# Mixer A: issuing the next chunk's matmuls ahead of the accumulation, with a lag of three states

## What is computed

```python
x_part, z = jnp.split(xn @ in_proj_w.T, 2, axis=-1)
u = jax.nn.silu(conv(x_part))                     # depthwise, 4 taps, 256 channels
dt, Bm, Cm = jnp.split(u @ x_proj_w.T, [8, 24], axis=-1)   # 8 ranks, 16 states
delta = jax.nn.softplus(dt @ dt_proj_w.T + dt_proj_b)
h = exp(delta * A) * h + delta * B * u            # for each step, channel and state
y = sum_over_states(h * C) + u * D
out = (y * jax.nn.silu(z)) @ out_proj_w.T
```

## Time and profile before

| | |
|---|---|
| median of 3 runs | 1151.61 us (1148.47 to 1152.67) |
| the profiled execution | 1151.89 us, span 1150.1 us |
| busy share of the span | PE 88%, DVE 65%, ScalarE 53%, POOL 50% |
| mean granted PE clock | 0.942 of full speed |
| mixer A | about 41 to 317 us of the span |

### The profile page before, as it was taken

One profiled execution on the slowest core, in us unless ns is written; L12 is line 12 of the kernel. 1 busy time (PEld: TensorE's weight loads), 2 busy tenths in 40 slices (PEclk: granted clock), 3 DMA queues, 4 the chain that ended last, 5 costly groups with the idle time before them and its releaser, 6 DMA issues. The chain is left out here.

```text
span 1150.1 us, 16414 instructions
## 1 busy us (share of the span) xinstructions
PE 1012.2 (88%) x4830; PEld 713.5 (62%) x4830; DVE 752.6 (65%) x1167; ACT 609.5 (53%) x1154; POOL 575.6 (50%) x455
## 2 busy tenths in 40 slices
PE   5988888868787989999999688896897899999997
PEld 2323323222255769999998345654575699999996
DVE  4788787998839755555555496655478555555555
ACT  5565463754254445555555586667542455555553
POOL 2378576685600687633741474621001887444732
PEclk9889889999979999999999987998988999999999
DMA  4222121222141214311111300000320133111103
GB/s 136 56 65 65 46 64 56 65 75 62 39 130 47 62 28 102 108 53 53 45 35 39 87 1 1 1 1 1 103 74 32 46 89 81 53 53 60 54 26 115
DMA packets 57248, 66.41 MB, mean 58 GB/s; under 512 B 6088, under 2 KB 40656, under 8 KB 57168
## 3 DMA queue, kind: packets, MB, share of 16 engines
q1 hardware_dynamic: 52176, 55.13, 15.9%
q0 software_dynamic: 4992, 10.23, 3.6%
HBM read 54.86 MB, written 10.49 MB: 57 GB/s over the span
## 5 line engine op out<-in xcount | busy, mean ns | idle before, releaser
L685 POOL TENSOR_TENSOR a_hc<-a_h,a_c_sb 128x512 f32<-128x512 f32 x128 | 160.1, 1267 | 94.3 <-DVE a_h L606 86.3
L417 PE MATMUL ps<-a_hc,eye 128*128 128x512 f32 x256 | 147.6, 684 | 24.1 <-POOL a_hc L685 23.6
L531 ACT ACTIVATE ps<-a_delta,a_neg_a 128x512 f32<-128x512 f32 x128 | 87.6, 688 | 111.4 <-DVE a_h L606 111.1
L417 PEld LDWEIGHTS ps<-a_hc,eye 128*128 128x128 f32 x256 | 45.1, 205 | 89.7 <-POOL a_hc L685 64.5
L590 DVE TENSOR_TENSOR a_b_u<-a_du,ps 128x1024 f32<-128x1024 f32 x64 | 77.2, 1206 | 35.9 <-PE ps L404 35.6
L877 POOL CAST g_ring_rounded<-g_ring 128x1876 fp32r<-128x1876 f32 x8 | 14.1, 1761 | 151.5 <-DVE g_table L1392 102.1
L606 DVE TENSOR_TENSOR_SCAN a_h<-ps,a_state,a_b_u 128x512 f32<-128x512 f32 x64 | 78.9, 1266 | 0.0
L1021 PE MATMUL ps<-g_ring_rounded,g_q_hi_rounded 128*128 x312 | 77.0, 337 | 0.0
L1021 PE MATMUL ps<-f_ring_rounded,f_q_hi_rounded 128*128 x312 | 77.0, 337 | 0.0
L606 DVE TENSOR_TENSOR_SCAN a_h<-ps,a_b_u 128x512 f32<-128x512 f32 x64 | 75.2, 1208 | 0.8 <-ACT ps L531 0.6
L877 POOL CAST f_ring_rounded<-f_ring 128x1876 fp32r<-128x1876 f32 x8 | 14.1, 1760 | 114.4 <-DVE f_table L1392 70.4
(11 more groups left out here) (450 smaller groups left out, 2865.8 us busy)
## 6 DMA issues: line engine op xcount, KB each, us to landing
a_c_sb<-c_rows SPq DMA_DIRECT2D x64, 256.0 KB, 3.3
f_ring<-in_gu SPq DMA_DIRECT2D x16, 469.0 KB, 4.5
g_ring<-in_gu SPq DMA_DIRECT2D x16, 469.0 KB, 4.4
f_ring<-in_dn SPq DMA_DIRECT2D x8, 512.0 KB, 6.6
g_ring<-in_dn SPq DMA_DIRECT2D x8, 512.0 KB, 5.7
xn_rows<-f_work SPq DMA_DIRECT2D x8, 256.0 KB, 2.6
f_rows<-token_rows SPq DMA_DIRECT2D x8, 256.0 KB, 5.0
xn_rows<-g_work SPq DMA_DIRECT2D x8, 256.0 KB, 2.6
```

The lines of the kernel that those rows point to most:

```text
L417: nc.tensor.matmul(ps[:, Y + f, :], k.eye[:, :], hc[:, s % DEPTH, :], start=False, stop=(n == NST - 1)).then_inc(y_added, 1)
L531: nc.scalar.activation(ps[:, A + m % NA, :], delta[:, f, cols(g)], ACT.Exp, scale=neg_a[:, f, n:n + 1])\
L685: nc.gpsimd.tensor_tensor(hc[:, s % DEPTH, :], h[:, s % DEPTH, :], c_sb[:, i % RING, :], ALU.mult)\
```

## The change

PE issues the next chunk's matmuls (`between`) ahead of the accumulation, and the accumulation runs three states behind the broadcasts instead of two. The product buffers `hc` become six, and POOL waits for the addition six steps before. DVE's gate comes after state 0 of the next chunk instead of state 1. Everything else is as before.

```diff
--- before.py
+++ after.py
@@ -255,6 +255,8 @@
 
     STEPS = NST * FT
     DEPTH = 4
+    WAITING = 6
+    LAG = 3
     RING = 4
     w_in = sb("w_in", [P, 2 * DI])
     w_tap = sb("w_tap", [P, FT, TAPS, P])
@@ -272,7 +274,7 @@
     c_rows = nc.dram_tensor("c_rows", (NST, T), F32, kind="Internal").ap()
     decayed_in = sb("b_u", [P, DEPTH, CH])
     h = sb("h", [P, DEPTH, CH])
-    hc = sb("hc", [P, DEPTH, CH])
+    hc = sb("hc", [P, WAITING, CH])
     c_sb = sb("c_sb", [P, RING, CH])
     state = sb("state", [P, STEPS])
     yz = sb("yz", [P, FT, CH])
@@ -414,7 +416,7 @@
                         u_done(g)
                         nc.tensor.matmul(ps[:, Y + f, :], skip[:, f, :], u[:, f, cols(g)], start=True, stop=False)
                     pe.wait_ge(hc_ready, s + 1)
-                    nc.tensor.matmul(ps[:, Y + f, :], k.eye[:, :], hc[:, s % DEPTH, :],
+                    nc.tensor.matmul(ps[:, Y + f, :], k.eye[:, :], hc[:, s % WAITING, :],
                                      start=False, stop=(n == NST - 1)).then_inc(y_added, 1)
 
             norm.of_tensor(pe)
@@ -439,11 +441,11 @@
             pe.wait_ge(z_first, FT)
             for m in range(NST * NCH):
                 broadcast(m)
-                if m >= 2:
-                    accumulate(m - 2)
                 between(*divmod(m, NST))
-            accumulate(NST * NCH - 2)
-            accumulate(NST * NCH - 1)
+                if m >= LAG:
+                    accumulate(m - LAG)
+            for m in range(NST * NCH - LAG, NST * NCH):
+                accumulate(m)
             in_turn(NCH, PROJECT)
 
         @block.scalar
@@ -607,7 +609,7 @@
                                              initial, ALU.mult, ALU.add).then_inc(scanned, 1)
 
             def between(g, n):
-                if g and n == 1:
+                if g and n == 0:
                     gate(g - 1)
                 if g and n == 4:
                     add(g - 1)
@@ -680,9 +682,9 @@
                     i = g * NST + n
                     if f == 0:
                         pool.wait_ge(c_loaded[i % RING], (i // RING + 1) * 16)
-                    if m >= DEPTH:
-                        pool.wait_ge(y_added, m - DEPTH + 1)
-                    nc.gpsimd.tensor_tensor(hc[:, s % DEPTH, :], h[:, s % DEPTH, :], c_sb[:, i % RING, :], ALU.mult)\
+                    if m >= WAITING:
+                        pool.wait_ge(y_added, m - WAITING + 1)
+                    nc.gpsimd.tensor_tensor(hc[:, m % WAITING, :], h[:, s % DEPTH, :], c_sb[:, i % RING, :], ALU.mult)\
                         .then_inc(hc_ready, 1)
                     if g + 1 < NCH:
                         if s == 21:
```

## The result

The changed kernel takes 1167.78 us (median of 4 runs, 1165.75 to 1170.99), the one before 1150.18 us (4 runs). The ratio is 1.0154, with a 95% interval of 1.0121 to 1.0187: slower by 17.6 us. The forecast was 1161.3 us with a range of 1143 to 1170, slower with a chance of 0.56; the measured time lies in that range, and 0.8 us above the 1156 to 1167 that the forecast gave its own mechanism.

A forecast was written before the change was run, and what follows sets the result against it. DVE was taken to bound mixer A. Its idle time was to go from 36.2 to 45.6 us, 9.4 us more, which added to 1151.9 us gave 1161.3 us, range 1143 to 1170.

The forecast's parts named there:

- Start: Start of chunk 0: DVE idles 1.5 us in place of 2.5 us before its fourth product.
- First dt projection and what follows it: Middle of three chunks: accumulation delays the broadcast, 2.24 us plus 2.5 us for slow clock, booked 4.8 us each.
- Second z projection: Three chunks: accumulation behind the wait for ScalarE's copy of z, 7.9 us plus 1.4 us each for clock.
- Gates: First two chunk boundaries: gate waits for the last state's accumulation, 4.55 us plus 2.5 us for clock, 7.05 us each.
- Output projection: Iteration 4 behind two boundaries: projection and accumulation delay the broadcast, 0.85 us plus 0.9 us for clock each.
- Third boundary: Last chunk boundary: no convolution in the gate's way, so zero wait.
- rival 2: PE slow after every gap, for as long as the chain lasts: 56.0 us of DVE idle, 1171.7 us; chance 0.12.
- Gaps over 4 us are slow: PE gaps over 4 us bring half pace for a mean 5.05 us, 2.5 us lost each.
- rival 1: Clock holds at 2.4 GHz at gate, dt and z projections: 26.9 us of DVE idle, 1142.6 us; chance 0.18.
- rival 3: Removed and new waits pay for each other: 34.6 us of DVE idle, 1150.3 us; chance 0.2.
- Rival 4: PE takes the accumulation in its slack, leaving only gains, up to 20.0 us at the boundaries: 1132 us; chance 0.03.

The follow-up runs named there:

- e2: Changed kernel with PE's old order, accumulation ahead of the next chunk's matmuls; lag three, six buffers, early gate kept: 1259.15 us, 0.9856 of the kernel before.
- e10: The kernel of e2 run again, beside its neighbours of another group: 1257.72 us, 0.9854 of the kernel before.
- e7: Changed kernel with four added matmuls ahead of PE's wait for each first dt projection, order unchanged: 1155.32 us, 1.0046 of the kernel before.
- e12: The changed kernel run again without edits, beside the other experiments: 1295.50 us, 1.0157 of the kernel before.
- e6: Changed kernel with the accumulation issued ahead of the second z projection in that iteration: 1162.11 us, 1.0099 of the kernel before.
- e4: Kernel before with six product buffers instead of four and nothing else: 1277.46 us, 0.9997 of the kernel before.
- e8: Changed kernel with the gate back after state 1: 1158.30 us, 1.0071 of the kernel before.
- e5: Changed kernel with the accumulation issued ahead of the second convolution in that iteration (state 2 of each chunk): 1152.32 us, 0.9999 of the kernel before.

## Why the prediction was right, and where it was off

**The direction and the cause held.** The forecast's mechanism, a ready accumulation between a late read of bank O and the broadcast, is shown by e2 and e10: order restored, nothing else, and the kernel goes from 1.6% slower to 1.5% faster. The clock as second factor is shown by e7.

**Terms of the sum, forecast against the first profile.** Start 1.5 us, measured 2.1. First dt projection and what follows it 14.4, measured 4.85 + 4.66 + 5.34 + 2.42 = 17.3. Second z projection 12.1, measured 12.5. Gates 14.1, measured 4.43 + 6.22 = 10.7. Output projection 3.5, measured 3.74 + 2.86 = 6.6. Third boundary 0, measured 0. Together 45.6, measured 49.1.

In e12 the same sum is 52.8 us, and the first two dt places are 8.3 and 8.1 us each. So the forecast was too low in both profiles, mostly by what the clock costs.

**What was mis-sized.** The gates, downward: the walk gave PE a gap of 4.3 us ahead of the second convolution, and it was 2.18 and 2.59 us. The halves of the first convolution, in iterations 0 and 1, keep PE busy, and I had left them out there; the clock held at the first gate, which stood 4.43 us, near the 4.55 us worked out for full clock, and fell only partly at the second. The output projection, upward: I gave its gap of 2.8 us a chance of 35% to lose the clock; the gap was 2.89 and 2.74 us, and both were followed by slow work. The dt projections, upward: that the slow stretch also makes the next broadcast late (2.42 us in the first profile, 2.96 and 2.85 in the second) was in no term. Smaller slips: 2.24 + 2.5 is 4.74 us and went in as 4.8; the 3.4 and 2.0 us in rival 2's boundaries come from no row; and in the earlier trace rows the matmul right behind the wait of 1.72 us still took 1.12 us, full pace, so that the slow stretch set in some 2 us later and not with it.

**How much of it was luck.** The total is 6.5 us above the forecast. In the changed kernel's first profile 1.5 us of that is mixer A (10.9 us more against 9.4) and 2.9 us the stages behind it, which the forecast took as unchanged; the rest lies between profile and medians. "Gaps over 4 us are slow" fitted all five such gaps of the first profile, but not as a rule. In e2 a gap of 4.18 us and in e12 one of 4.22 us were followed by a dt projection at or near full pace (1.12 and 1.27 us), and the clock fell only behind it. The gap of 2.18 us ahead of the first gate was followed by full pace in the changed kernel; at the same length it was followed in e6 by a convolution half of 3.52 us, and the gate waited 5.96 us there. In the same place of the unchanged order, a gap of 3.03 us was followed by full pace before and by half pace in e4 (waits of 4.21 and 7.13 us). So a forecast of single clock falls was a matter of odds; the sum over some ten places came near.

The Trainium skill, "TensorE: Matmul & The Clock Gate", section on HAM oscillation, has every burst after such a wait start cold. For the six dt and z gaps of 3.9 to 5.4 us in the changed kernel's first profile the trace agrees; after the 2.18 us gap the clock held, and e12's gap of 4.22 us and e2's of 4.18 us differ from it. Rival 2 went by that rule, at 1171.7 us, and the measured 1167.8 lies between it and the forecast, nearer to rival 2. DVE's idle time decides better than the total: 49.1 us is nearer to the forecast's 45.6 than to rival 2's 56.0, and e12's 52.8 is nearer to rival 2. The kernel lies between the two.

**The rivals.** The clock did not hold (rival 1), except at the first gate and in part at the second. The loss and gain did not cancel (rival 3). Rival 4, waits that don't show, is refuted by nine waits for L406 of over 2 us each.

**What stands behind mixer A.** The forecast had it unchanged. In the profiles it is 832.19 us before and 835.12 after, 2.9 us more. In the windows view, a stretch of mixer B and the whole rest, before:

```profile
637.91:717.91 80.00, 61.94 (x244) 35.45 (x243) 53.28 (x72) 54.99 (x95) 42.93 (x37) 0.85 0.05 15
...
317.91:1150.10 832.19, 753.94 (x4350) 624.76 (x4350) 497.96 (x930) 443.03 (x870) 380.61 (x297) 0.95 0.19 55
```

and the same distances from mixer A's end, after:

```profile
648.78:728.78 80.00, 62.05 (x237) 34.59 (x238) 52.48 (x72) 54.30 (x91) 42.32 (x36) 0.83 0.06 15
...
328.78:1163.90 835.12, 756.51 (x4350) 626.00 (x4350) 497.96 (x930) 443.04 (x870) 380.53 (x297) 0.95 0.19 54
```

Busy times hardly differ and the granted clock in mixer B is 0.85 against 0.83. From the last addition to x to the end it is 832.5 in before, 832.4 in e7, 833.6 in e8, 835.1 in e6, 835.4 in e5 and 835.5 in the changed kernel. Kernels of the same order fall on both sides, so it may be chance in where the clock falls, which no run settles. It also stays open why the medians are 17.6 us apart and the two profiles only 13.9. The changed kernel's profile was its fastest run, and its second profile had a mixer A 3.8 us longer; that would fill the difference but is argued, not shown.

## What to carry to other kernels

In an engine that works in order, look at what stands between an instruction that waits late and the next one that the bound engine needs, and issue ready work ahead of the wait, never behind it. More lag and more buffers give room only if the order lets the engine use it: here the same lag, buffers and early gate were worth 1.5% with one order and cost 1.6% with the other. Swap two statements at one place at a time; one swap (e5) gave back the whole loss, though the two-statement swap everywhere (e2, e10) is worth twice as much.

## What the hardware showed beyond that

A gap of 2.9 us was followed by 5.7 us at 1.2 GHz, one of 2.1 us was not, and in the earlier trace rows one of 3.1 us was not: the length alone doesn't tell. PE's timeline of e6 has the changed kernel's gap ahead of the first gate once more, 2.19 us long, and here the half convolution took 3.52 us in place of 1.99:

```profile
118.03 3.52 PE L334 MATMUL ps<-a_xp,a_w_tap 128*128 128x512 f32 x4 [2.19 <-ACT a_u L492]
```

Twelve matmuls that nobody needs made a kernel 12.5 us faster. In its profile they kept PE's clock up in two of three gaps, and mixer A accounts for 7.2 us of the gain.

On the chip of the first and third group the kernel before took 126 us more. The waits behind mixer A (total, times, longest) of the changed kernel on the first chip and then there (e12) point to the loads of the experts' weights:

```profile
POOL g_ring_rounded L879 <- DMA g_ring<-in_dn: 49.5, 4, 17.4
...
POOL f_ring_rounded L879 <- DMA f_ring<-in_dn: 44.4, 3, 17.9
```

```profile
POOL g_ring_rounded L879 <- DMA g_ring<-in_dn: 82.9, 5, 20.0
...
POOL f_ring_rounded L879 <- DMA f_ring<-in_dn: 76.9, 5, 17.5
```

POOL waited 82.9 us for the loads that cost it 49.5 us on the first chip (for those of the first expert stage it was 76.9 and 44.4 us). That is 66 us of the 126; where the rest lies was not followed, and what makes the loads late there was not tried. Mixer A, which loads little, took 276.5 us there with six buffers against 273.75 us here.
